# A decoder layer over 64 sequences: VectorE's chains in single calls, all call lists drawn up anew, two waits of GpSimd left out

## The chip, the cores and the metric

One core of a Trainium2 chip runs the whole kernel in one launch. The metric is the device time in microseconds, from the kernel's start to its end; lower is better. The engines of the core are named as the profile names them: PE (TensorE), DVE (VectorE), ACT (ScalarE), POOL (GpSimd) and SP (SyncE, whose queue carries the DMAs).

## The reference

Each of 64 sequences has 256 tokens of 256 channels (`x`) and a context of 120 tokens (`ctx`). All three parts end in a residual sum and a layer norm:

```python
# 1. mixer (a state-space layer, 8 heads of 64)
z, xBC, dt = split(x @ W_in.T)
dt  = softplus(dt + dt_bias)
xBC = silu(causal_conv4(xBC) + conv_b);  xs, B, C = split(xBC)
y   = ssd(xs * dt, -exp(A_log) * dt, B, C) + xs * D      # = (exp(segsum) * C B^T) (xs dt)
y   = y * silu(z);  y = y * rsqrt(mean(y*y) + 1e-5) * norm_w
x1  = layernorm(x + y @ W_out.T)
# 2. cross attention: queries from x1, keys and values from [ctx, x1] (376 rows), 8 heads
x2  = layernorm(x1 + softmax(q k^T / 8) v @ Wout)
# 3. coupling net, three cycles over all 256 channels of each token
gf  = sigmoid(gelu(gelu(mean_tokens(x2) @ g1) @ g2) @ g3)
out = x2
for _ in range(3):
    tf = sigmoid(gelu(gelu(gelu(out @ c1) @ c2) @ c3) @ c4)
    out = out + (0.1 + r * (0.7*gf + 0.3*tf - 0.5) * 2) * twist(out)
result = layernorm(out)
```

`twist` permutes the four quarters of the channels and changes two signs.

## The kernel before

All tensors of one sequence fit on the chip, so nothing is tiled over DMA beyond loading a sequence and storing it. The work is a software pipeline over sequences, written out by hand. In the iteration `p` of the steady loop the coupling net works on `f = p - 2`, attention on `a = p - 1`, the mixer on `m = p`, and the projections of `m + 1` are begun. Each engine has its own in-order list of calls: PE's loop is at L630 to L701, ACT's at L1195 to L1276, DVE's at L1929 to L2002, POOL's at L2296 to L2319, and SP's at L2457 to L2471, each between a list for the first sequences and one for the last. There is no scheduler: an engine runs its list from the top and stops wherever a semaphore that the call needs is not up. The semaphores count calls, so the same call may stand elsewhere in the list as long as its buffers allow.

PE writes to eight PSUM banks: bank 0 for the coupling net, a ring of three for scores, one of two for queries, keys, values and turned probabilities, one of two for the mixer (L234). A bank is free when the reader named in `freed` has counted up; with two or three banks a late reader on DVE or ACT stops PE two or three calls later.

The calls that the text speaks of, by PE's list:

- `scores(s, c, i)` (L418): four products of one head pair, which use 64 of the array's rows each (`r = slice(k * HD, (k + 1) * HD)`). DVE takes the row maximum (`top`, L1638), ACT exponentiates (`exp`, L979), PE turns the result (`turn`, L431), and ACT (L989) and DVE (L1657) take turns at copying it from PSUM.
- `values(s, c)` (L442) and `y_pair(s, q)` (L316): products that write 64 of the array's columns each.
- `layer(s, cyc, n)` (L479): layer `n` of the coupling net in cycle `cyc`; L497, L503 and L512 are its products, L1021, L1023 and L1025 ACT's gelus, L1033 the tanh that stands for the sigmoid. Between two cycles DVE runs `cycle` (L1708): the coupling (L1716), its product with the twisted part (L1721 or L1727), and the sum (L1724 or L1729). PE's next layer (L497) waits for the gelu of that sum (L1021).
- `x2_turn(s)` (L468, its instructions at L475): the start of the coupling net of a sequence, once per sequence.
- On DVE: `taps` (L1440, its instructions at L1442), three dependent additions of the convolution; `norm` (L1416), the statistics of a layer norm; `out_sum` (L1731), three dependent steps; and so on. In each of them a step waits for the one before it, on DVE itself.
- On POOL: `masked` (L2119), the causal mask over the decay matrix `Lm`; `times_g` (L2130), `Lm` times `C B^T`, which `y_pair` waits for; `factors` (L2198), the small numbers that `out_sum` needs; `ffn` and `att`, reciprocal roots for the layer norms.

Two waits on POOL have no data behind them. `times_g(m + 1, 0, summed=f)` waits until DVE has finished `out_sum(f, 1)`, and `factors(f, divided=a)` waits until DVE has multiplied the attention output by the reciprocals (L1666).

ACT holds one set of function tables at a time. The exponential, the gelu, the logarithm of softplus and the tanh with the exponential are in different sets, and where its list goes from one to another an `ACT_TABLE_LOAD` stands: seven in each sequence.

## Time and profile before

| | |
|---|---|
| median of 3 runs | 3865.07 us (3864.32 to 3865.35) |
| span of the profiled execution | 3861.4 us |
| around the span | 3.7 us against the median |
| PE, DVE, ACT, POOL busy | 98%, 85%, 84%, 45% |
| chain that ended last, by engine | PE 59%, ACT 16%, DVE 15%, POOL 4%, issue 4% |
| `ACT_TABLE_LOAD` | 1.283 us each, 189 ahead of `exp`, 125 ahead of the gelu |

The time of the profiled execution is its span of 3861.4 us and what lies around it; the median of the runs is 3.7 us above the span. The busy times of the engines come from the same execution. A busy share of 98% means that the engine had an instruction in it, not that every instruction took its least possible time: matmuls overlap, and the time from the start of one group to the start of the next is what a group costs.

### The profile page before, as it was taken

How to read it: one execution, taken by the hardware profiler on the slowest of the kernel's cores; microseconds unless marked ns; L12 is line 12 of the kernel's file. 1: busy time of each engine (PE TensorE's matmuls, PEld its weight loads, DVE VectorE, ACT ScalarE, POOL GpSimd, SP SyncE). 2: the span in 40 equal slices, each digit the busy share in tenths (PEclk: the TensorE clock that was granted, in tenths of full speed). 3: DMA queues.
4: the chain of work that ended last, by engine and by line, in shares of the span. 5: the costliest groups of instructions: out<-in, count | busy, mean ns of one | idle time of the engine just before them, and what ended most of it. 6: DMA issues, size and time to landing. Idle time of an engine off the chain costs nothing.

```text
span 3861.4 us, 77375 instructions
## 1 busy us (share of the span) xinstructions
PE 3783.3 (98%) x25728; PEld 3000.9 (78%) x25728; DVE 3286.2 (85%) x8098; ACT 3237.9 (84%) x7812; POOL 1748.5 (45%) x3084
## 2 busy tenths in 40 slices
PE   6999999999999999999999999999999999999997
...
GB/s 97 54 47 59 55 45 61 54 42 58 58 45 55 48 59 54 45 61 53 43 57 59 45 55 50 56 55 45 61 55 42 61 55 45 55 54 53 55 38 17
DMA packets 312350, 203.14 MB, mean 53 GB/s; under 512 B 55056, under 2 KB 310928, under 8 KB 311952
## 3 DMA queue, kind: packets, MB, share of 16 engines
...
## 4 chain that ended last, share of the span: by engine, by line
PE 59%; ACT 16%; DVE 15%; issue 4%; POOL 4%; DMA 1%; SPq 0%; DVEq 0%; POOLq 0%
PE psum L253 20%; PE psum L428 8%; PE psum L338 6%; PE psum L463 5%; PE psum L438 5%; PE psum L452 4%; PE psum L325 4%; ACT prob L979 3%; ACT h L1021 2%; ACT L979 2%; ACT L1021 2%; PE psum L497 2%; ACT xc L891 2%; POOL rs_mix L2175 2%; DVE nmax L1638 1%
## 5 line engine op out<-in xcount | busy, mean ns | idle before, releaser
L979 ACT ACTIVATE prob<-psum,nmax 128x376 f32<-128x376 f32 x1024 | 585.2, 575 | 49.5 <-DVE nmax L1638 46.2
L1638 DVE TENSOR_REDUCE nmax<-psum 128x1 f32<-128x376 f32 x1024 | 541.5, 540 | 14.4 <-PE psum L428 11.0
L2139 POOL TENSOR_TENSOR Lm<-Lm,G 128x384 f32<-128x384 f32 x512 | 506.1, 1012 | 92.8 <-DVE out_sb L1741 68.4
L438 PE MATMUL psum<-ident,prob 128*128 128x128 f32 (+1 forms) x3072 | 480.5, 276 | 2.1 <-ACT probT L989 1.1
L1442 DVE SCALAR_TENSOR_TENSOR u<-psum,par,u 128x253 f32<-128x253 f32 (+5 forms) x960 | 449.1, 479 | 28.1 <-ACT u L882 1.7
L428 PE MATMUL psum<-kT,q_sb 64*128 64x376 f32 x2048 | 467.7, 528 | 0.2 <-ACT prob L979 0.2
L438 PEld LDWEIGHTS psum<-ident,prob 128*128 128x128 f32 (+1 forms) x3072 | 363.0, 141 | 73.9 <-issue 45.0
L989 ACT ACTIVATE probT<-psum 128x384 f32<-128x384 f32 x512 | 252.7, 494 | 182.7 <-PE psum L438 182.5
L2126 POOL TENSOR_SCALAR_AFFINE_SELECT Lm<-Lm 128x256 f32<-128x256 f32 x512 | 205.7, 435 | 411.6 <-DMA Lm<-cum_row 411.6
L253 PE MATMUL psum<-x_hi,w_in_hi 128*128 128x256 f32 (+1 forms) x1152 | 360.9, 313 | 22.5 <-DVE w_in_lo L1764 9.3
L452 PE MATMUL psum<-probT,V 128*64 128x256 f32 (+1 forms) x3072 | 375.0, 385 | 0.3 <-ACT probT L989 0.3
L253 PE MATMUL psum<-x_hi,w_in_lo 128*128 128x256 f32 (+1 forms) x1152 | 326.0, 283 | 0.0
L253 PE MATMUL psum<-x_lo,w_in_hi 128*128 128x256 f32 (+1 forms) x1152 | 325.4, 283 | 0.0
L452 PEld LDWEIGHTS psum<-probT,V 128*64 128x64 f32 (+1 forms) x3072 | 202.4, 136 | 134.5 <-ACT probT L989 33.0
L1657 DVE COPY probT<-psum 128x384 f32<-128x384 f32 x512 | 279.9, 547 | 31.4 <-PE psum L438 27.2
L2194 POOL TENSOR_TENSOR h_a<-h_a,cpl 128x512 f32<-128x512 f32 x64 | 82.0, 1281 | 492.3 <-DVE h_pre L1724 492.3
L915 ACT ACTIVATE Lm<-Lm,ncum 128x256 f32<-128x256 f32 x512 | 262.8, 513 | 0.7 <-DVE ncum L1533 0.7
L463 PE MATMUL psum<-wo_sb,oT 128*128 128x256 f32 x1024 | 248.3, 386 | 0.7 <-DVE oT L1666 0.7
L979 ACT ACT_TABLE_LOAD x189 | 242.5, 1283 | 3.3
L338 PE MATMUL psum<-w_out_sb,g 128*128 128x256 f32 x1024 | 237.8, 386 | 0.0
L253 PEld LDWEIGHTS psum<-x_hi,w_in_hi 128*128 128x128 f32 (+1 forms) x1152 | 215.0, 187 | 28.4 <-issue 12.8
L463 PEld LDWEIGHTS psum<-wo_sb,oT 128*128 128x128 f32 x1024 | 189.4, 190 | 58.7 <-issue 32.9
...
## 6 DMA issues: line engine op xcount, KB each, us to landing
...
invT<-inv_row SPq DMA_DIRECT2D x256, 128.0 KB, 3.0
...
inv_row<-inv_t SPq DMA_DIRECT2D x512, 1.0 KB
...
```

The source lines that it names most:

```text
L253: t = mm(dst, a, b, start=n == 1, stop=n == 3 * KT)
L338: t = mm(banks[b][:, i * D:(i + 1) * D], g[:, c, i * P:(i + 1) * P], w_out_sb[:, c, :], start=c == 0, stop=c == CT - 1)
L428: mm(banks[b][:, 0:NK], q_sb[r, c, i * P:(i + 1) * P], kT[r, c, :], start=True, stop=True).then_inc(p_sc, 1)
L438: t = tr(banks[b][0:m, j * P:(j + 1) * P], prob[:, r, j0:j0 + m], ident[:, :])
L452: t = mm(banks[b][k * HD:(k + 1) * HD, 0:L], V[0:m, j, h * HD:(h + 1) * HD], probT[0:m, (8 * s + h) % HP, j, :], start=j == 0, stop=j == l ...
L463: t = mm(banks[b][:, 0:D], oT[:, c, i * P:(i + 1) * P], wo_sb[:, c, :], start=c == 0, stop=c == CT - 1)
L915: act(Lm[:, h, 0:L], Lm[:, h, 0:L], ACT.Exp, bias=ncum[:, 0, h:h + 1])
L979: act(prob[:, r, :], b[:, 0:NK], ACT.Exp, bias=nmax[:, n:n + 1], accum_out=psum_row[:, n:n + 1]).then_inc(a_exp, 1)
L1442: stt(u[0:rows, c, d:L], src[:, 0:L - d], prm("conv_w", 4 * c + 3 - d, slice(0, rows)), u[0:rows, c, d:L], ALU.mult, ALU.add).then_inc(don ...
L1638: e.tensor_reduce(nmax[:, n:n + 1], banks[bank_of["sc", s, n]][:, 0:NK], AX.X, ALU.max, negate=True).then_inc(d_max, 1)
L1657: cp(probT[:, (8 * s + 2 * c + k) % HP, :, i * P:(i + 1) * P], b[:, 0:len(JT) * P].rearrange("p (j t) -> p j t", j=len(JT))).then_inc(d_tn, 1)
L2139: t = tt(Lm[:, h, :], Lm[:, h, :], G[:, :], ALU.mult)
```

## The change

1. DVE's functions are cut into single instructions, each with the semaphore it needs: `taps` into `tap` (called by `conv_tap(s, c, n)` and `bcdt_tap(s, n)`), `norm` into `row_stats` and `row_mean`, `cycle` into `gain`, `twisted_part` and `pre`, `out_sum` into `out_x` and `out_tw`, and in the same way `cum`, `by_token`, `x1_raw`, `x1_norm`, `x1_keep`, `kv_split`, `inverse` and `x2_split`. Their arithmetic is the same, and so is the number of instructions.
2. The lists of all five engines, for the first sequences, the steady loop and the last ones, are written in another order. PE's steady list now begins at another place in the period. SP starts the load of the first context behind those of the weights.
3. The two waits of POOL are left out.
4. A few semaphores follow from it: a bank of `bcdt` is free only when its taps are done too, `conv_th` waits for two channels' own counts, and the first spreading of the sums waits for the weights.

```diff
-                freed[b] = [(d_dta, s + 1)]
+                freed[b] = [(d_dta, s + 1), (d_uB, 3 * s + 3)]
...
-            def taps(src, c, rows, done, at):
-                for n, d in enumerate((1, 2, 3)):
-                    stt(u[0:rows, c, d:L], src[:, 0:L - d], prm("conv_w", 4 * c + 3 - d, slice(0, rows)),
-                        u[0:rows, c, d:L], ALU.mult, ALU.add).then_inc(done, 1)
-                    if n < 2:
-                        ve.wait_ge(done, at + n + 1)
...
+            def tap(src, c, rows, n, done, s):
+
+                d = n + 1
+                ve.wait_ge(done, 3 * s + n)
+                stt(u[0:rows, c, d:L], src[:, 0:L - d], prm("conv_w", 4 * c + 3 - d, slice(0, rows)),
+                    u[0:rows, c, d:L], ALU.mult, ALU.add).then_inc(done, 1)
+
+            def bcdt_tap(s, n):
+                if not live(s):
+                    return
+                ve.wait_ge(a_uB, s + 1)
+                tap(banks[bank_of["bcdt", s]][0:TAIL, 0:L], CT, TAIL, n, d_uB, s)
...
-            def cycle(s, cyc):
-
-                if not live(s):
-                    return
-                n = FD * s + 3 * cyc
-                c_all = cpl[:, cyc, :].unsqueeze(1).broadcast_to([P, KT, L])
+            def gain(s, cyc):
+
+                if not live(s):
+                    return
                 ve.wait_ge(a_f, FA * s + 6 + 5 * cyc)
                 ve.wait_ge(d_base, s + 1)
                 ts(cpl[:, cyc, :], cpl[:, cyc, :], tf_gain[:, :], c_cyc[:, :], ALU.mult, ALU.add).then_inc(d_f, 1)
-                ve.wait_ge(d_f, n + 1)
+
+            def twisted_part(s, cyc):
+
+                if not live(s):
+                    return
+                ve.wait_ge(d_f, FD * s + 3 * cyc + 1)
+                ve.wait_ge(d_x2, 2 * s + 2)
+                ve.wait_ge(a_hb, s + 1)
+                c_all = cpl[:, cyc, :].unsqueeze(1).broadcast_to([P, KT, L])
                 if cyc == 0:
-                    ve.wait_ge(d_x2, 2 * s + 2)
-                    ve.wait_ge(a_hb, s + 1)
                     tt(h_pre[:, :, :], h_b[:, :, :], c_all, ALU.mult).then_inc(d_f, 1)
-                    ve.wait_ge(a_ha, s + 1)
-                    ve.wait_ge(d_f, n + 2)
-                    tt(h_pre[:, :, :], h_pre[:, :, :], h_a[:, :, :], ALU.add).then_inc(d_f, 1)
                 else:
                     ve.wait_ge(l_tw, 2 * s + 2)
                     tt(h_b[:, :, :], h_b[:, :, :], c_all, ALU.mult).then_inc(d_f, 1)
-                    ve.wait_ge(d_f, n + 2)
-                    tt(h_pre[:, :, :], h_pre[:, :, :], h_b[:, :, :], ALU.add).then_inc(d_f, 1)
-
-            def out_sum(s, i):
+
+            def pre(s, cyc):
+
+                if not live(s):
+                    return
+                ve.wait_ge(a_ha, s + 1)
+                ve.wait_ge(d_f, FD * s + 3 * cyc + 2)
+                tt(h_pre[:, :, :], h_pre[:, :, :], (h_b if cyc else h_a)[:, :, :], ALU.add).then_inc(d_f, 1)
...
+            def out_x(s, i):
...
+                ts(out_sb[:, i, :], x2[:, s % 2, i, :], of_x[:, i:i + 1], None, ALU.mult).then_inc(d_out[i], 1)
+
+            def out_tw(s, i, k):
+
+                if not live(s):
+                    return
+                ve.wait_ge(d_out[i], 3 * s + 1)
                 x2_, o = x2[:, s % 2, i, :], out_sb[:, i, :]
-                ts(o, x2_, of_x[:, i:i + 1], None, ALU.mult).then_inc(d_out[i], 1)
-                ve.wait_ge(d_out[i], 3 * s + 1)
-                stt(o[:, 0:P], x2_[:, P:D], of_tw[:, i:i + 1], o[:, 0:P], ALU.mult, ALU.add).then_inc(d_out[i], 1)
-                stt(o[:, P:D], x2_[:, 0:P], of_minus[:, i:i + 1], o[:, P:D], ALU.mult, ALU.add).then_inc(d_out[i], 1)
+                to, of_, by = ((slice(0, P), slice(P, D), of_tw), (slice(P, D), slice(0, P), of_minus))[k]
+                stt(o[:, to], x2_[:, of_], by[:, i:i + 1], o[:, to], ALU.mult, ALU.add).then_inc(d_out[i], 1)
...
-            def times_g(s, q, summed=None):
-
-                if not live(s):
-                    return
-                if summed is not None:
-                    po.wait_ge(d_out[1], 3 * summed + 3)
+            def times_g(s, q):
+
+                if not live(s):
+                    return
...
-            def factors(s, divided=None):
+            def factors(s):
...
-                if divided is not None:
-                    po.wait_ge(d_o, 2 * divided + 2)
...
                 sp.wait_ge(d_cum, s + 1)
+                sp.wait_ge(set_w, 3)
                 sp.wait_ge(cum_in, 32 * (s - 1))
```

PE, mid kernel, around the products of `Lm` (`y_pair`, L325 before and L326 now) and the scores (L428, now L429). Before:

```order
L438 MATMUL psum<-ident,prob 120x128
L438 MATMUL psum<-ident,prob 128x128 x2
L325 MATMUL psum<-Lm,xdt 64x256 x2
L325 MATMUL psum<-Lm,xdt 64x128 x2
L325 MATMUL psum<-Lm,xdt 64x256 x2
L325 MATMUL psum<-Lm,xdt 64x128 x2
L428 MATMUL psum<-kT,q_sb 128x376 x2
L438 MATMUL psum<-ident,prob 120x128
L438 MATMUL psum<-ident,prob 128x128 x2
L438 MATMUL psum<-ident,prob 120x128
L438 MATMUL psum<-ident,prob 128x128 x2
```

and now:

```order
L439 MATMUL psum<-ident,prob 128x128 x2
L429 MATMUL psum<-kT,q_sb 128x376 x2
L326 MATMUL psum<-Lm,xdt 64x256 x2
L326 MATMUL psum<-Lm,xdt 64x128 x2
L326 MATMUL psum<-Lm,xdt 64x256 x2
L326 MATMUL psum<-Lm,xdt 64x128 x2
L429 MATMUL psum<-kT,q_sb 128x376 x2
L326 MATMUL psum<-Lm,xdt 64x256 x2
L326 MATMUL psum<-Lm,xdt 64x128 x2
L326 MATMUL psum<-Lm,xdt 64x256 x2
L326 MATMUL psum<-Lm,xdt 64x128 x2
L429 MATMUL psum<-kT,q_sb 128x376 x2
```

Between the scores and the two halves of `y_pair`'s work no turn (L438, now L439) stands any more; seven calls that use half of the array follow one another.

DVE at the end of the coupling net's first cycle: `cpl`, `h_pre` are the coupling's, `u` is the convolution (L1442 before, L1451 now). Before:

```order
L1706 SCALAR_TENSOR_TENSOR c_cyc<-tg,gf_gain,c_base 128x1
L1716 TENSOR_SCALAR cpl<-cpl,tf_gain,c_cyc 128x256
L1721 TENSOR_TENSOR h_pre<-h_b,cpl 128x512
L1724 TENSOR_TENSOR h_pre<-h_pre,h_a 128x512
L1442 SCALAR_TENSOR_TENSOR u<-psum,par,u 128x255
L1442 SCALAR_TENSOR_TENSOR u<-psum,par,u 128x254
L1442 SCALAR_TENSOR_TENSOR u<-psum,par,u 128x253
L1442 SCALAR_TENSOR_TENSOR u<-psum,par,u 128x255
L1442 SCALAR_TENSOR_TENSOR u<-psum,par,u 128x254
L1442 SCALAR_TENSOR_TENSOR u<-psum,par,u 128x253
L1430 TENSOR_SCALAR ctx_n<-ctx_sb,mv_ctx,rs_ctx 120x256
```

and now:

```order
L1677 TENSOR_TENSOR kv_lo<-kv,kv_hi 128x2x256
L1670 CAST kv_hi<-kv 128x2x120
L1773 TENSOR_SCALAR cpl<-cpl,tf_gain,c_cyc 128x256
L1451 SCALAR_TENSOR_TENSOR u<-psum,par,u 128x255
L1677 TENSOR_TENSOR kv_lo<-kv,kv_hi 128x2x120
L1451 SCALAR_TENSOR_TENSOR u<-psum,par,u 128x255
L1784 TENSOR_TENSOR h_pre<-h_b,cpl 128x512
L1451 SCALAR_TENSOR_TENSOR u<-psum,par,u 128x254
L1795 TENSOR_TENSOR h_pre<-h_pre,h_a 128x512
L1451 SCALAR_TENSOR_TENSOR u<-psum,par,u 128x254
L1684 TENSOR_REDUCE nmax<-psum 128x1
L1451 SCALAR_TENSOR_TENSOR u<-psum,par,u 128x253
```

The two runs of three dependent taps are taken apart, and the steps of the coupling and of the split of `kv` stand between them.

ACT where the projections' softplus (`dt_e`) meets the first gelus (`h`, L1021 before and L1026 now). Before:

```order
L989 ACTIVATE probT<-psum 128x3x128
L870 ACTIVATE dt_e<-dt_e 8x256
L872 ACT_TABLE_LOAD
L872 ACTIVATE dt_e<-dt_e,ones 8x256
L1021 ACT_TABLE_LOAD
L1021 ACTIVATE h<-psum,par 128x256 x2
L969 ACTIVATE V<-psum 128x512
L1043 ACTIVATE h_a<-psum 128x512
L979 ACT_TABLE_LOAD
```

and now:

```order
L1012 ACTIVATE h_pre,x2sum<-psum 128x256 x2
L874 ACTIVATE dt_e<-dt_e 8x256
L876 ACT_TABLE_LOAD
L876 ACTIVATE dt_e<-dt_e,ones 8x256
L896 ACT_TABLE_LOAD
L896 ACTIVATE xc<-u 128x512
L984 ACTIVATE prob,psum_row<-psum,nmax 128x376
L1048 ACTIVATE h_a<-psum 128x512
L1063 ACT_TABLE_LOAD
L1063 ACTIVATE g<-psum,par 128x1
L1026 ACTIVATE h<-psum,par 128x256 x2
```

The first half of the convolution's tanh (`xc`, L896) now stands behind the softplus and needs a table of its own, so a sequence has eight table loads and not seven.

POOL behind the last of the factors (`of_minus`), where the two waits were. Before:

```order
L2225 TENSOR_SCALAR of_x<-of_x 128x2
L2226 TENSOR_SCALAR of_minus<-of_tw 128x2
L2139 TENSOR_TENSOR Lm<-Lm,G 128x384 x2
L2126 AFFINE_SELECT Lm<-Lm 128x2x128 x2
L2139 TENSOR_TENSOR Lm<-Lm,G 128x384 x2
L2115 TENSOR_SCALAR ve_ffn<-mv_ffn 128x1
L2117 TENSOR_TENSOR rs_ffn<-ve_ffn,minus_half 128x1
L2115 TENSOR_SCALAR ve_ffn<-mv_ffn 128x1
L2117 TENSOR_TENSOR rs_ffn<-ve_ffn,minus_half 128x1
L2139 TENSOR_TENSOR Lm<-Lm,G 128x384 x4
```

and now:

```order
L2529 TENSOR_SCALAR of_x<-of_x 128x2
L2530 TENSOR_SCALAR of_minus<-of_tw 128x2
L2445 TENSOR_TENSOR Lm<-Lm,G 128x384 x8
L2423 TENSOR_SCALAR ve_ffn<-mv_ffn 128x1
L2425 TENSOR_TENSOR rs_ffn<-ve_ffn,minus_half 128x1
L2455 TENSOR_TENSOR g<-xc,gate 128x256
L2423 TENSOR_SCALAR ve_ffn<-mv_ffn 128x1
L2425 TENSOR_TENSOR rs_ffn<-ve_ffn,minus_half 128x1
```

All eight products with `G` (L2139, now L2445) follow the factors in one run, and the masks stand before them.

## Rows read from the trace of the kernel before

**Rows 1.** Page, part 1: busy us, share of the span, instructions of each engine.

```profile
PE 3783.3 (98%) x25728; PEld 3000.9 (78%) x25728; DVE 3286.2 (85%) x8098; ACT 3237.9 (84%) x7812; POOL 1748.5 (45%) x3084
```

**Rows 2.** Windows: stretch, length, busy us (count) of PE, PEld, DVE, ACT, POOL, clock.

```profile
0.00:60.00 60.00, 30.78 (x148) 25.14 (x148) 45.13 (x116) 31.28 (x57) 22.07 (x39) 0.80 0.52 155
60.00:120.00 60.00, 52.94 (x345) 40.93 (x346) 45.78 (x113) 39.47 (x98) 22.20 (x31) 0.94 0.04 11
120.00:3780.00 3660.00, 3641.74 (x24920) 2892.27 (x24921) 3155.79 (x7776) 3128.46 (x7562) 1684.26 (x2960) 1.00 0.18 52
3780.00:3862.00 82.00, 57.88 (x319) 42.61 (x315) 39.54 (x95) 38.69 (x96) 19.97 (x54) 0.82 0.06 17
```

**Rows 3.** Turning of `x` into channels (L475): durations, first and last start, two stretches.

```profile
L475 PE MATMUL psum<-ident,x x4: 271/272/273, 146.0 to 146.3; 128*128 128x128 f32 x4
...
L475 PE MATMUL psum<-ident,x x8: 270/272/273, 3683.3 to 3741.4; 128*128 128x128 f32 x8
```

**Rows 4.** Waits of PE, largest group: line, releaser, us in total, times, longest.

```profile
PE psum L497 <- ACT h L1021: 19.0, 64, 3.6
```

**Rows 5.** Timeline of PE, mid kernel: start us, us, instruction, count [idle before <-releaser].

```profile
1516.91 1.52 PE L452 MATMUL psum<-probT,V 120*64 120x256 f32 x12
1518.36 0.38 PE L527 MATMUL psum<-g,gw_sb 128*128 128x1 f32 x2
...
1524.86 1.52 PE L452 MATMUL psum<-probT,V 120*64 120x256 f32 x12
1526.41 1.10 PE L497 MATMUL psum<-h,cw_sb 128*128 128x256 f32 x4
...
1528.81 0.49 PE L438 MATMUL psum<-ident,prob 128*120 128x128 f32 x3
1529.27 0.44 PE L253 MATMUL psum<-kv_hi,wkv_hi 128*128 128x376 f32 x1
...
1530.40 0.61 PE L512 MATMUL psum<-h,cw_row 128*128 128x128 f32 x4
1530.84 0.49 PE L438 MATMUL psum<-ident,prob 128*120 128x128 f32 x3
1531.09 0.36 PE L253 MATMUL psum<-x_hi,w_in_hi 128*128 128x256 f32 x1
...
1535.36 0.49 PE L438 MATMUL psum<-ident,prob 128*120 128x128 f32 x3
1536.04 1.10 PE L497 MATMUL psum<-h,cw_sb 128*128 128x256 f32 x4 [0.20 <-ACT h L1021]
...
1538.35 2.81 PE L452 MATMUL psum<-probT,V 120*64 120x256 f32 x24
1541.10 0.39 PE L509 MATMUL psum<-cw_col,h 128*128 128x2 f32 x2
```

**Rows 6.** Timeline of DVE, the same period.

```profile
1525.24 2.94 DVE L1442 SCALAR_TENSOR_TENSOR u<-psum,par,u 128x255 f32<-128x255 f32 x6
...
1528.41 0.73 DVE L1604 TENSOR_SCALAR x<-x_pre,mv_mix,rs_mix 128x256 f32<-128x256 f32 x2
...
1531.85 0.41 DVE L1716 TENSOR_SCALAR cpl<-cpl,tf_gain,c_cyc 128x256 f32<-128x256 f32 x1 [1.18 <-ACT cpl L1033]
1532.30 0.69 DVE L1727 TENSOR_TENSOR h_b<-h_b,cpl 128x512 f32<-128x512 f32 x1
```

**Rows 7.** Table loads of ACT at `exp`: count, busy us, mean ns, idle before.

```profile
L979 ACT ACT_TABLE_LOAD x189 | 242.5, 1283 | 3.3
```

**Rows 8.** Waits of POOL: the first of the two that the change concerns.

```profile
POOL c_col L2215 <- DVE oT L1666: 223.6, 61, 4.8
```

**Rows 9.** Page, part 5: products with `G` on POOL, with the second wait.

```profile
L2139 POOL TENSOR_TENSOR Lm<-Lm,G 128x384 f32<-128x384 f32 x512 | 506.1, 1012 | 92.8 <-DVE out_sb L1741 68.4
```

**Rows 10.** Groups of DVE, normalising calls of one shape: count, busy us, mean ns.

```profile
L1430 DVE TENSOR_SCALAR out_sb<-out_sb,mv_ffn,rs_ffn 128x256 f32<-128x256 f32 x128 | 93.7, 732 | 30.5 <-POOL rs_ffn L2117 30.5
...
L1430 DVE TENSOR_SCALAR x<-x,mv_att,rs_att 128x256 f32<-128x256 f32 x128 | 52.2, 408 | 1.2 <-POOL rs_att L2117 1.2
```

1807 lines of the change are left out of this document (1053 added, 754 removed).

## The prediction

> **What bounds the kernel now.** I read the page's busy shares first: PE is busy for 98% of the span, DVE for 85%, ACT for 84%, POOL for 45% [rows 1]. Next the windows, because a share over the whole span mixes the ends with the middle. In the 3660 us from 120 to 3780 PE is busy for 3641.74, so it is idle for 18; in the first 120 us it is idle for 29 + 7 = 36, in the last 82 for 24 [rows 2]. Then the period: the first `x2_turn` starts at 146.0, the 61st at 3683.3, so 60 periods take 3537.3 us and one takes 58.96 [rows 3]; the middle window holds 62 of them. Per period ACT is busy for 3128.46/62 = 50.5 and DVE for 3155.79/62 = 50.9: eight us of slack on each. The bound is PE's own list. The waits confirm it: the largest group, the first layer of a cycle behind ACT's gelu, is 19.0 us in 64 times [rows 4].
>
> So only two things can shorten the period: what PE's calls cost in their order, and the stalls still in it. The groups' start-to-start times show both, where durations don't, since matmuls overlap [rows 5]:
> - A head pair's values cost 1518.36 - 1516.91 = 1.45 us. Two values calls with nothing between them (x24) cost 1541.10 - 1538.35 = 2.75, not 2.90. Half-array calls next to each other save 0.15 per joint.
> - Stalls: values take 1.55 before the next layer and not 1.45 (0.10); the turn at 1528.81 takes 0.46 where the one at 1530.84 takes 0.25 (0.21: a bank is still held); the turn at 1535.36 takes 0.68, of which 0.25 is its own and 0.43 lies before the gelu, 0.20 of it named by the profile. Together 0.74 per period; other, smaller ones I can't tell from the calls' cost.
>
> **PE's new order.** I counted the half-array calls (scores, values, `y_pair`) in both steady lists, and how often they stand together. Before they form ten groups in a period: the scores of (0,1), (1,0), (1,1), (3,0) and (m,0,0) alone, `y_pair` 0 and 1 behind scores, `y_pair` 2 and 3 ahead of scores, scores with values 0, values 1 alone, values 2 and 3. Now there are six: values 2 and 3 with scores (0,1); scores (1,0); the seven calls around `y_pair`; scores (3,0); values 0 and 1 with scores (3,1); scores (m,0,0). Four groups fewer, at 0.15: 0.60 us less. The calls moved away from between them still run, and each starts behind a call of another kind as before, so I book nothing for them. That is 0.60 x 61 = 37 us.
>
> Below, this could be nothing, if the joint of the x24 row belongs to two values calls alone and scores beside `y_pair` save nothing (only two of the four joins are of values). Above, it is 0.7, if entering from a turn costs more than the 0.15.
>
> The Trainium skill speaks against part of it. "TensorEngine Tiling (Array Packing)", section Key Properties, says that changing the tiling mode, not only the tile, drains TensorE. Scores split the rows and values and `y_pair` split the columns, so by that rule a change between them inside a group costs too: three such changes before, six now. Counted in changes of any kind that is 23 before and 18 now, and the saving would be half of an entry-and-exit pair's 0.15 times five, 0.38 us per period or 23 us, not 37. No row shown here separates the two; it is a rival below.
>
> **The stalls.** The stall at 1536.04 sits on a chain. PE's third layer starts at 1530.40; DVE's coupling starts 1.45 later (1.18 of it idle, waiting for the tanh), its three steps of 0.41, 0.69 and again 0.69 with their gaps take 1.86 [rows 6]; then ACT loads a table, 1.28 [rows 7], computes the gelu, and PE starts 2.33 after DVE's last step: 5.64 in all. In the new list PE places other calls of 4.98 us between the same two layers (one K tile, two `xcT`, the next scores, two turns, a z projection, at their start-to-start times). If the table were loaded behind DVE's last step again, PE would stand still for 0.66. But between ACT's tanh and the gelu now stand only one K copy and one `exp`, so the load runs beside DVE's steps: 5.64 - 1.28 = 4.4 at best; with the K copy and the exponential waiting for PE's K tile it is nearer 4.9. I take a stall of 0.1 to 0.2 here. At the first gelu of the sequence ACT's list has become longer by one load (eight per sequence, one behind softplus): + 1.28 x 61 on ACT, which lifts it from 50.5 to 51.8 of 58 and hides in its slack except there; between `x2_turn`'s end and that layer PE has about 3.2 us of other calls, ACT about 2.8 with the load (both added up by me from the timelines of before, an estimate). So it is tight in two places, and loose in most others, because DVE answers sooner (next part). Of the 0.74 I take 0.5 to remain: -0.24 x 61 = -14 us.
>
> Bounds: all of it goes (-45 us), or the new order's own stalls are 0.3 us above the old (+18 us).
>
> **VectorE in single steps.** Six taps in two dependent runs take 2.94 us; two independent calls of 0.41 take 0.73 from start to end, a pitch of 0.32 against (2.94 - 0.48)/5 = 0.49 for calls of 0.48 [rows 6]. A neighbour that waits for the one before starts 0.01 behind its end; one that doesn't starts 0.08 ahead of it. That is about 0.1 per dependent pair. By my count some 33 pairs stand side by side in a period before and 5 now: 2.8 us of DVE's time per period. DVE is not the bound, so this alone is worth nothing; what it does is to bring row maxima and copies forward, and I have put that into the stalls. Cost if the cover fails: a step now spread over other instructions ends later than it did (the three taps of one channel now have six other instructions among them), which `conv_th` and the turns behind it would feel; the slack of eight us covers it.
>
> **GpSimd's two waits.** They cost POOL (223.6 + 68.4)/61 = 4.8 us per period [rows 8, 9], on an engine that is idle for more than half. What they kept apart is now together: eight products `Lm` x `G` of 1.01 us [rows 9], about 8 us in one run, start as DVE's `out_x` and `out_tw` do. DVE's normalising of `out_sb`, which ran beside such products, takes 732 ns on average, and the same call on `x`, which mostly didn't, 408 [rows 10]. If six DVE calls of a period each lose 0.3 so, DVE is 1.9 us later there, against 2.8 won. I book zero on PE, with the loss as the rival on the slower side.
>
> **The ends.** The first context is now loaded behind the weights, and DVE's first statistics wait for it; the casts of the query and key weights come early on ACT. PE's 36 us of idle in the first 120 hold both a gain and a loss: the later projections need no cast in the middle, the first taps may wait for the context. The closing chain behind the last `x2_turn` is the same. I take 0, bounds -8 and +8.
>
> **Sum.** 3861.4 - 37 - 14 + 0 = 3810.4, and with the 3.7 us by which the median stands above the profiled span, 3814; rounded for the smaller unnamed gains and losses I say 3815.
>
> **The rivals.**
> - *The stalls go altogether.* For it: DVE 2.8 us freer, POOL 4.8; against it: the two tight places on ACT. -(0.6 + 0.74) x 61 = -82: 3783.
> - *The gain is eaten or was never there.* Either each change of split inside a group costs as much (-23 and no stalls won: 3842), or the joins save only where values meet values and the gelu's chain, with its added load, holds the period near 58.9: about 3862, no change. This is also the case in which the change does not do what it says, since freeing DVE moves nothing that PE waits for.
> - *Slower.* POOL's one run of eight products lies on DVE's `out_x`, `out_tw`, the statistics and `x_low`. Behind these stand the row maxima for the scores of (1,0) and (1,1); the ring for scores has three banks, so PE stops as soon as DVE is later than about 1 us with a maximum. Six calls at up to 0.65 (twice the mean surcharge of 0.32, if half of the 128 calls of rows 10 were hit) are 4 us on DVE in that stretch, where the freed pairs give back little; beyond the 1 us that the ring covers, up to 3 us can reach PE. I take 1.3 of them: with 0.84 won elsewhere, +0.46 x 61 = +28, which is 3893. It decides from 0.84 + 0.13 = 0.97 us per period of new waits on. For it speaks the 732; against it, that in all of the old lists' periods PE never lost more than 0.43 us at one place though DVE waited 1.18 in it [rows 5, 6].
>   The Trainium skill, "SBUF — State Buffer", section "SBUF: two separate sides", calls the port pair shared by the two engines an exclusive lock that whoever starts first keeps for the whole instruction, for DVE calls with two SBUF inputs among others. By that, `out_tw` could wait for a whole product of 1 us each: four of them, 4 us, the same end of the scale.
>
> **Chances.** The forecast 0.52, stalls gone 0.15, gain eaten 0.19 (of it 0.13 faster, 0.06 no change), slower 0.14. A measurement tells 0.2%, 7.7 us, from no change, so: faster 0.80, same 0.06, slower 0.14. The range goes from the stall-free case, 3783, to just past no change, 3866; about 0.15 lies above it and 0.04 below.
>
> **What would show it.** The period between two `x2_turn` should be 58.1 us (58.96 - 0.84). Right or wrong step by step: the seven calls around `y_pair` start to start at their single costs less 0.15 a joint; the wait of the first layer behind the gelu, 19.0 us in all, smaller; eight table loads a sequence; DVE's busy time lower by some 2.8 x 62 = 170 us minus what POOL costs it (the pairs' gaps are short, so part shows as idle time instead); POOL's two waits gone and `out_x` and `out_tw` longer than before. The forecast is wrong if scores inside the long group start 0.1 or more late behind `y_pair`, if PE waits over 0.5 us a period for row maxima, or if DVE's calls beside the eight products take 0.7 us each.

## The result, and the profile after

The changed kernel takes 4256.33 us (median of 4 runs, 4248.81 to 4264.10) against 3864.70 of the kernel before: ratio 1.101, 95% interval 1.0996 to 1.103. It is slower by 391 us where 50 us less was forecast, and far above the range of 3783 to 3866.

The profiled execution is 4262.3 us long and the slowest of the four. First the page's part 1 and two windows (columns as in [rows 1, 2]):

```profile
PE 3826.6 (90%) x25728; PEld 3049.7 (72%) x25728; DVE 3508.3 (82%) x8098; ACT 3318.3 (78%) x7873; POOL 1782.4 (42%) x3084
```

```profile
0.00:60.00 60.00, 21.41 (x119) 18.21 (x120) 37.08 (x96) 26.76 (x52) 22.12 (x37) 1.00 0.39 117
120.00:4180.00 4060.00, 3696.76 (x24968) 2948.58 (x24967) 3385.31 (x7786) 3212.91 (x7631) 1716.86 (x2960) 0.99 0.16 47
```

PE is busy for 90% and not 98% [rows 1]; nothing became full. In the middle PE stood still for 363 of 4060 us, where it was 18 of 3660 [rows 2]. DVE's busy time rose by 222 us for the same 8098 instructions; some 170 us less was expected, minus what POOL costs. The starts of the coupling net (L476 now; the two stretches of [rows 3]):

```profile
L476 PE MATMUL psum<-ident,x x4: 270/272/273, 156.9 to 157.2; 128*128 128x128 f32 x4
```

and, near the end,

```profile
L476 PE MATMUL psum<-ident,x x12: 270/272/273, 4082.6 to 4187.1; 128*128 128x128 f32 x12
```

The first is 11 us later than before, the 61st at 4082.6: a period of (4082.6 - 156.9)/60 = 65.43 us, 6.47 above the 58.96 of before. Sixty such periods are 388 us; the head adds 11, the tail 2: together the 401 us between the two spans (the medians are 391 apart). So the loss is in the steady loop. The waits of PE say who ends the idle time (line, releaser, us in total, times, longest):

```profile
PE psum L439 <- DVE x L1726: 135.0, 59, 2.6
PE psum L498 <- ACT h L1026: 120.5, 66, 3.6
PE psum L313 <- DVE xc L1513: 56.3, 63, 1.6
```

Against 19.0 us for the largest group before [rows 4] there are three of 56 to 135, each about once per sequence: a turn that needs the bank of the output projection, which DVE's residual sum (L1726) frees; the third cycle's first layer behind the gelu; the mixer's transposes behind DVE's silu. In PE's timeline of one period they stand at three places:

```profile
2013.46 0.63 PE L313 MATMUL psum<-ident,xc 128*128 128x128 f32 x4 [0.72 <-DVE xc L1513]
...
2020.89 1.10 PE L498 MATMUL psum<-h,cw_sb 128*128 128x256 f32 x4 [1.84 <-ACT h L1026]
...
2025.08 2.82 PE L453 MATMUL psum<-probT,V 120*64 120x256 f32 x24
2027.83 0.90 PE L429 MATMUL psum<-kT,q_sb 64*128 64x376 f32 x4
...
2033.97 0.90 PE L429 MATMUL psum<-kT,q_sb 64*128 64x376 f32 x4
2037.43 0.54 PE L439 MATMUL psum<-ident,prob 128*120 128x128 f32 x3 [2.56 <-DVE x L1726]
...
2040.90 0.49 PE L439 MATMUL psum<-ident,prob 128*120 128x128 f32 x3
2041.32 0.90 PE L429 MATMUL psum<-kT,q_sb 64*128 64x376 f32 x4
2042.15 1.52 PE L326 MATMUL psum<-Lm,xdt 128*64 128x256 f32 x16
2043.60 0.90 PE L429 MATMUL psum<-kT,q_sb 64*128 64x376 f32 x4
```

All three end in DVE. DVE's timeline of the same period:

```profile
2010.27 0.89 DVE L1481 SCALAR_TENSOR_TENSOR th<-th,u 16x256 f32<-16x256 f32 x1
2011.17 1.42 DVE L1482 SCALAR_TENSOR_TENSOR th<-th,u 16x256 f32<-16x256 f32 x1
...
2017.94 0.41 DVE L1773 TENSOR_SCALAR cpl<-cpl,tf_gain,c_cyc 128x256 f32<-128x256 f32 x1
...
2026.74 0.69 DVE L1716 TENSOR_TENSOR oT<-oT,invT 128x512 f32<-128x512 f32 x1 [2.85 <-DMA invT<-inv_row]
2029.22 0.69 DVE L1716 TENSOR_TENSOR oT<-oT,invT 128x512 f32<-128x512 f32 x1 [1.78 <-ACT oT L1003]
...
2030.94 1.07 DVE L1803 TENSOR_SCALAR out_sb<-x,of_x 128x256 f32<-128x256 f32 x1 [0.57 <-POOL of_minus L2530]
2032.05 0.97 DVE L1812 SCALAR_TENSOR_TENSOR out_sb<-x,of_tw,out_sb 128x128 f32<-128x128 f32 x1
2032.95 1.08 DVE L1812 SCALAR_TENSOR_TENSOR out_sb<-x,of_minus,out_sb 128x128 f32<-128x128 f32 x1
...
2035.08 0.96 DVE L1812 SCALAR_TENSOR_TENSOR out_sb<-x,of_tw,out_sb 128x128 f32<-128x128 f32 x1
2035.96 0.41 DVE L1426 BATCH_NORM_STATS2 st_ffn<-out_sb 128x6 f32<-128x256 f32 x1
2036.30 0.74 DVE L1812 SCALAR_TENSOR_TENSOR out_sb<-x,of_minus,out_sb 128x128 f32<-128x128 f32 x1
2036.96 0.74 DVE L1726 TENSOR_TENSOR x<-psum,x 128x256 f32<-128x256 f32 x2
```

and POOL's:

```profile
2009.60 1.28 POOL L2500 TENSOR_TENSOR h_a<-h_a,cpl 128x512 f32<-128x512 f32 x1
2010.96 1.35 POOL L2502 TENSOR_TENSOR h_b<-h_b,h_a 128x512 f32<-128x512 f32 x1
...
2030.87 7.03 POOL L2445 TENSOR_TENSOR Lm<-Lm,G 128x384 f32<-128x384 f32 x7
```

Read them side by side. From 2030.87 POOL runs seven products on end; DVE's six calls of the output sum take 0.74 to 1.08 us each, about one per product, while a call of the statistics between them (L1426) takes its usual 0.41, and the residual sum starts at 2036.96. (The eighth product waits 4 us for ACT.) From 2009.60 POOL runs the twist; DVE's two silu calls take 0.89 and 1.42. And from 2024 to 2029 DVE, whose list has come to the division, stands still twice. The groups over the whole span, of after and then of the kernel before (count, busy us, mean ns, idle before):

```profile
L1803 DVE TENSOR_SCALAR out_sb<-x,of_x 128x256 f32<-128x256 f32 x128 | 125.3, 980 | 26.8 <-POOL of_minus L2530 26.0
L1812 DVE SCALAR_TENSOR_TENSOR out_sb<-x,of_tw,out_sb 128x128 f32<-128x128 f32 x128 | 118.1, 924 | 4.3
L1812 DVE SCALAR_TENSOR_TENSOR out_sb<-x,of_minus,out_sb 128x128 f32<-128x128 f32 x128 | 111.7, 873 | 0.0
...
L1482 DVE SCALAR_TENSOR_TENSOR th<-th,u 16x256 f32<-16x256 f32 x64 | 85.9, 1342 | 0.9
...
L1481 DVE SCALAR_TENSOR_TENSOR th<-th,u 16x256 f32<-16x256 f32 x64 | 62.7, 979 | 1.0 <-ACT th L868 1.0
```

```profile
L1741 DVE SCALAR_TENSOR_TENSOR out_sb<-x,of_minus,out_sb 128x128 f32<-128x128 f32 x128 | 53.8, 420 | 0.0
...
L1740 DVE SCALAR_TENSOR_TENSOR out_sb<-x,of_tw,out_sb 128x128 f32<-128x128 f32 x128 | 47.1, 368 | 4.6
L1738 DVE TENSOR_SCALAR out_sb<-x,of_x 128x256 f32<-128x256 f32 x128 | 46.9, 367 | 76.4 <-POOL of_minus L2226 76.3
...
L1473 DVE SCALAR_TENSOR_TENSOR th<-th,u 16x256 f32<-16x256 f32 x64 | 26.7, 417 | 0.9
L1472 DVE SCALAR_TENSOR_TENSOR th<-th,u 16x256 f32<-16x256 f32 x64 | 26.1, 408 | 0.0
```

The output sum costs 355.1 us where it cost 147.8, the two silu calls 148.6 where they cost 52.8: 207 and 96 us, 4.7 us per sequence of VectorE's time, paid for leaving GpSimd's work beside it.

Behind its long waits PE also loses clock. In another period it stood still for 1.83 us until 1628.55 and for 2.46 until 1646.32, and the windows behind show the granted clock at its lower level, 1.2 GHz instead of 2.4 (columns as above, the clock third from the end):

```profile
1630.20:1633.40 3.20, 3.20 (x17) 3.20 (x16) 1.01 (x2) 2.02 (x4) 0.35 (x2) 0.50 0.48 125
1647.30:1650.50 3.20, 3.20 (x14) 3.20 (x14) 3.20 (x12) 1.93 (x6) 0.00 (x0) 0.50 0.02 5
```

In the trace of before there is no such stretch between 120 us and the 61st `x2_turn`; here 24 of the 60 periods have one or more and last 66.11 us on average, the other 36 last 64.97. An estimate from the two: (65.43 - 64.97) x 60, some 28 of the 401 us, go with the clock. No run separates them from the waits in front of them.

### The profile page after: what moved, and what is told of

The parts are those of the page before. It is cut to its first block, busy times and chain, and to the rows that moved or that the text cites. A ratio compares the mean times of both kernels' runs of the same rounds, so it can differ in the third digit from the quotient of the medians.

```text
span 4262.3 us, 77876 instructions
## 1 busy us (share of the span) xinstructions
PE 3826.6 (90%) x25728; PEld 3049.7 (72%) x25728; DVE 3508.3 (82%) x8098; ACT 3318.3 (78%) x7873; POOL 1782.4 (42%) x3084
## 4 chain that ended last, share of the span: by engine, by line
PE 55%; DVE 26%; issue 7%; ACT 5%; SPq 3%; DMA 2%; POOL 2%; POOLq 0%; DVEq 0%; ACTq 0%
PE psum L254 19%; PE psum L439 7%; PE psum L429 7%; PE psum L339 5%; DVE out_sb L1812 5%; PE psum L326 4%; PE psum L453 4%; DVE out_sb L1803 3%; PE psum L498 3%; DMA invT<-inv_row 2%; DVE probT L1707 2%; SPq L2706 1%; PE psum L504 1%; DVE th L1481 1%; DVE xc L1513 1%
## 5 line engine op out<-in xcount | busy, mean ns | idle before, releaser
L439 PE MATMUL psum<-ident,prob 128*128 128x128 f32 (+1 forms) x3072 | 517.0, 285 | 136.8 <-DVE x L1726 135.0
L2445 POOL TENSOR_TENSOR Lm<-Lm,G 128x384 f32<-128x384 f32 x512 | 518.5, 1042 | 286.3 <-ACT Lm L921 267.8
L1684 DVE TENSOR_REDUCE nmax<-psum 128x1 f32<-128x376 f32 x1024 | 548.3, 536 | 46.3 <-PE psum L429 44.0
L439 PEld LDWEIGHTS psum<-ident,prob 128*128 128x128 f32 (+1 forms) x3072 | 360.7, 146 | 295.9 <-DVE x L1726 172.1
L429 PE MATMUL psum<-kT,q_sb 64*128 64x376 f32 x2048 | 483.5, 528 | 0.5 <-ACT kT L965 0.5
L1451 DVE SCALAR_TENSOR_TENSOR u<-psum,par,u 128x255 f32<-128x255 f32 (+5 forms) x960 | 433.0, 468 | 35.2 <-ACT u L886 29.3
L2434 POOL TENSOR_SCALAR_AFFINE_SELECT Lm<-Lm 128x256 f32<-128x256 f32 x512 | 227.0, 481 | 541.4 <-DMA Lm<-cum_row 541.4
L254 PE MATMUL psum<-x_hi,w_in_hi 128*128 128x256 f32 (+1 forms) x1152 | 355.1, 308 | 24.9 <-DVE u L1451 10.8
L453 PE MATMUL psum<-probT,V 128*64 128x256 f32 (+1 forms) x3072 | 360.8, 383 | 2.2 <-ACT probT L994 2.2
L1716 DVE TENSOR_TENSOR oT<-oT,invT 128x512 f32<-128x512 f32 x128 | 91.9, 718 | 319.1 <-DMA invT<-inv_row 245.1
L2515 POOL TENSOR_TENSOR cd<-c_col 128x2 f32<-128x2 f32 x64 | 12.5, 196 | 734.3 <-DMA c_col<-c_row 734.3
L498 PE MATMUL psum<-h,cw_sb 128*128 128x256 f32 x768 | 210.6, 397 | 120.7 <-ACT h L1026 120.5
L429 PEld LDWEIGHTS psum<-kT,q_sb 64*128 64x128 f32 x2048 | 172.0, 184 | 126.9 <-issue 93.4
```

What stands on the lines that cost most here:

```text
L254: t = mm(dst, a, b, start=n == 1, stop=n == 3 * KT)
L429: mm(banks[b][:, 0:NK], q_sb[r, c, i * P:(i + 1) * P], kT[r, c, :], start=True, stop=True).then_inc(p_sc, 1)
L439: t = tr(banks[b][0:m, j * P:(j + 1) * P], prob[:, r, j0:j0 + m], ident[:, :])
L453: t = mm(banks[b][k * HD:(k + 1) * HD, 0:L], V[0:m, j, h * HD:(h + 1) * HD], probT[0:m, (8 * s + h) % HP, j, :], start=j == 0, stop=j == l ...
L498: t = mm(b[:, 0:L], cw2_sb[:, k, :], h1[:, k, :], start=k == 0, stop=k == KT - 1)
L1451: stt(u[0:rows, c, d:L], src[:, 0:L - d], prm("conv_w", 4 * c + 3 - d, slice(0, rows)), u[0:rows, c, d:L], ALU.mult, ALU.add).then_inc(don ...
```

## The experiments

Each ran beside the kernel before on the same chip, which took 3863.9 to 3865.5 us. Most are medians of two executions that lie up to 14.5 us apart (e4), so differences of a few us between two of them say nothing. "Less" and "slower" are against the changed kernel or the run that is named. Edits are shown in part, without the context.

**Waits put back (e1).**

```diff
+                if summed is not None and summed >= 0:
+                    po.wait_ge(d_out[1], 3 * summed + 3)
...
+                if divided is not None and divided >= 0:
+                    po.wait_ge(d_o, 2 * divided + 2)
```

> The changed kernel with GpSimd's two waits put back where they stood: its first product of a sequence waits for the first half of the output sum, and its factors wait for the division. Theory A (the waits kept GpSimd's products off VectorE's output sum; without them the six calls take 0.87 to 0.98 us instead of 0.37 to 0.42, 3.2 us a period, and the turn behind the residual sum stands still for 2.4): three of six calls are short again, some 1.6 us of 65.5 a period come back, but the factors start 1 us later because the division itself is late, so 0.5 to 1.5 us a period or 30 to 90 us less: 4170 to 4230. Theory B (the lists themselves put the division too late, behind a DMA that SyncE issues late, and this sets the period): no gain or a loss up to 1.3 us a period, 4256 to 4335.

4156.11 us, 100 less: somewhat more than theory A asked for. The division and the factors come late, but four of the six calls are short again, the three that the wait covers and the one that starts before the first product; the other two take 0.97 and 0.74 us in the timeline.

**Products behind both halves (e2).**

```diff
+                    po.wait_ge(d_out[1], 3 * summed + 3)
+                    po.wait_ge(d_out[0], 3 * summed + 3)
```

> The changed kernel with one wait for GpSimd: its eight products start only when both halves of VectorE's output sum are done; the factors don't wait. Theory A: the six calls of the output sum are back at 0.37 to 0.42 us, VectorE is 3.2 us earlier at the residual sum, the stall of the turn behind it (2.4 us a period) goes: 2.0 to 3.0 us a period less, 4070 to 4135. Theory B: VectorE catches up elsewhere and PE stands still at the next late place, 4220 to 4256; slower than 4256 if the products now come too late for the mixer's products.

4096.63 us, 160 less, inside theory A's range. The six calls are short, and the wait of 135 us for the residual sum is gone from the list of PE's waits; the gelu's stays:

```profile
L1803 DVE TENSOR_SCALAR out_sb<-x,of_x 128x256 f32<-128x256 f32 x128 | 45.4, 356 | 30.7 <-POOL of_minus L2533 30.1
```

```profile
PE psum L498 <- ACT h L1026: 120.8, 66, 3.6
```

**The two waits left out of the old lists (e3).**

```diff
-                factors(f, divided=a)
+                factors(f)
-                times_g(m + 1, 0, summed=f)
+                times_g(m + 1, 0)
```

> The kernel before with nothing changed but GpSimd's two waits left out (the third part of the change alone). Theory A: the output sum's six calls get slower here too, by up to 2 us a period where the old list has only two products in a row, and VectorE's slack takes half: 3865 to 3980, with the output sum's mean above 0.5 us. Theory B: the waits matter little in either order, 3855 to 3875.

3871.57 us, ratio 1.0018 (1.0006 to 1.0029). The output sum does get slower (589, 359 and 728 ns on average), but PE loses only 7 us. In the old list two products stand there, in the new one eight.

**Thin products (e4).**

```diff
-                    t = tt(Lm[:, h, :], Lm[:, h, :], G[:, :], ALU.mult)
+                    t = tt(Lm[:, h, 0:8], Lm[:, h, 0:8], G[:, 0:8], ALU.mult)
```

> The changed kernel with GpSimd's eight products per sequence cut to 8 of their 384 columns (the rest of the product with C B^T is left out, so the result is another): it takes away nearly all that they can hold VectorE up with, and makes them early. Theory A: output sum back at 0.37 to 0.42 us, 2.4 to 3.2 us a period less, 4060 to 4110. Theory B: 4220 or more. What remains above 58 us a period in this run is the price of the lists and of the other GpSimd work.

4056.37 us: 200 less. Of these 160 are what e2 gives back. No run splits the other 40: here the products also come early, and `x_low` (L1445), which e2's late products hold up to 1218 ns on average, takes 681.

**Reciprocals early (e5), on top of e2.** In SP's list:

```diff
                 spread_cum(a)
+                spread_inv(f - 1, 0)
...
-                spread_inv(f - 1, 0)
                 load_x(a)
```

> As e2_products_later (4097 us; output sum undisturbed), and SyncE issues the spreading of the first half of the attention reciprocals right behind that of the decay sums, some 30 us earlier, instead of behind the coupling rows. Theory A (where the transfers for the division stand in SyncE's list sets the division, which holds VectorE): VectorE's wait for them, 216 us in all, goes and 1 to 2 us a period with it: 3980 to 4040. Theory B (the division would wait for ACT's copy of the attention output and the output sum for the factors anyway): VectorE's wait moves to those, PE gains at most its 0.3 at the output projection: 4075 to 4097.

4096.77 us: no change, as theory B said. DVE's wait has another name:

```profile
DVE oT L1716 <- ACT oT L1003: 297.9, 62, 5.7
```

The division would have waited for ACT's copy of the attention output anyway.

**Twist first (e6), on top of e2.** In POOL's list:

```diff
+                twist(f - 2)
                 masked(a, 0)
...
                 masked(a, 3)
-                twist(f - 2)
```

> As e2_products_later, and GpSimd computes the two steps of the twist before the masks and not behind them, so that they no longer lie on VectorE's two calls for silu of B and C (0.96 and 1.34 us where they took 0.41 and 0.42). Theory A (this is the same contention, at a second place): the two calls are back near 0.42, PE's wait of 1.0 us a period at the mixer's transposes goes and some of the 2.0 us before the third cycle's first layer: 1.0 to 2.0 us a period, 3975 to 4035. Theory B (the order of VectorE's list sets both): under 0.3 us a period, 4080 to 4097.

4060.32 us, 36 less than e2: little more than half of the least that theory A gave. PE's wait at the transposes (L313) is gone from its list. The two calls fall to 576 and 526 ns, not to 0.42: the masks now lie on them.

**Coupling first (e7), on top of e2.**

```diff
                 by_token(a)
-                bc_high(a)
-                x1_keep(f, 0)
                 x_dt(a, 0)
-                bc_low(a)
                 gain(f - 2, 1)
                 twisted_part(f - 2, 1)
                 pre(f - 2, 1)
+                bc_high(a)
+                x1_keep(f, 0)
+                bc_low(a)
```

> As e2_products_later, and in VectorE's list the three steps of the second cycle's coupling stand ahead of the splitting of B and C (eight small calls) and not behind it. Theory A (contention alone): the chain to the gelu still starts late, under 0.5 us a period, 4065 to 4097. Theory B (VectorE's list asks for the coupling 2.5 us later than ACT has its tanh ready, and PE's 2.0 us before the third cycle's first layer are the price): 1.5 to 2.2 us a period less, 3960 to 4005, with PE's wait for the gelu near the 19 us of the kernel before.

4051.14 us, 45 less than e2, half of the least that theory B gave. PE's wait for the gelu went from 120.8 us to 11.9, below the 19 of the kernel before; but a new one took most of it:

```profile
PE psum L303 <- DVE xdt L1576: 72.6, 60, 2.2
```

Part of the 45 is the clock: from 120 to 4000 us the granted clock is 1.00 here and 0.99 in e2. e2's periods without a stretch at the lower clock last 62.18 us and e7's 61.85, 0.33 less, where the means of all periods differ by 0.78 (62.69 and 61.91).

**The three together (e8).** The edits of e5, e6 and e7 on top of e2.

> The edits of e5, e6 and e7 together on top of e2. If they are separate places the gains add up: the known stalls left are then those before the mixer's output projection (0.5 to 0.9 us), before a K tile (0.4) and small ones, so 59.5 us a period and 3890 to 3930. If they hide one another, it is no better than the best of the three by more than 20 us.

4029.71 us: 67 below e2, where the single gains are 0, 36 and 45. It missed the 3890 to 3930 of adding up; by the other branch of the expectation, the places hide one another. The wait at L303 is now 105.1 us: what is called earlier makes something else late. Whether DVE is simply full there, e12 decides.

**Dependent neighbours taken apart in the old lists (e9).** Taps of two channels alternate; `gain`, the twisted part and the sum stand between taps; the two steps of `x2_split` stand between the taps of B, C and dt.

```diff
-                bcdt(m + 1)
-                x2_split(f)
+                bcdt_and_split(m + 1, f)
                 softplus(m + 1)
-                conv(m + 1, 0)
-                conv(m + 1, 1)
+                conv_two(m + 1, 0)
...
-                cycle(f, 0)
-                conv(m + 1, 2)
-                conv(m + 1, 3)
+                cycle_and_conv(f, m + 1)
```

> The kernel before, with all its lists, where only VectorE's dependent neighbours are taken apart in the steady loop: the taps of two channels alternate, the coupling's three steps stand between taps, the split of x2 between the taps of B, C and dt (14 of some 33 dependent pairs a period). The first part of the change alone. Theory A (VectorE isn't the bound; its freed 1 to 1.5 us a period are worth nothing to PE): within 0.1%, 3861 to 3869. Theory B (the kernel before loses time to these pairs on the chain to the gelu): 0.2 to 0.35 us a period less, 3843 to 3852.

4021.88 us, ratio 1.040 (1.0387 to 1.0422): 156 us slower than the kernel before, and neither theory had it. DVE's timeline:

```profile
1992.58 0.43 DVE L1734 CAST x2T_hi<-h_pre 128x512 fp32r<-128x512 f32 x1 [1.51 <-ACT h_pre L1007]
...
1994.92 1.27 DVE L1461 SCALAR_TENSOR_TENSOR dt_e<-dt_a 8x256 f32<-8x256 f32 x1
...
2012.87 0.41 DVE L1779 TENSOR_SCALAR cpl<-cpl,tf_gain,c_cyc 128x256 f32<-128x256 f32 x1 [1.34 <-ACT u L882]
```

The cast of `x2` was put between two taps and waits 1.51 us for ACT, and the two taps that could have run wait behind it. The coupling was put behind the wait for the convolution's input, 1.34 us. And what came later met GpSimd: L1461 takes 1.27 us for its 0.42. PE's wait for the gelu (L497) is 125.9 us where it was 19.0.

**Seven table loads (e10), on top of e8.** On ACT, and on DVE (`x_silu`):

```diff
-                conv_th(m + 1, 0)
-                exp(a, 11)
                 keep_a(f)
...
                 layer(f, 0, 2)
+                exp(a, 11)
+                conv_th(m + 1, 0)
                 exp(a, 12)
...
-                x_silu(a, 0)
...
                 kv_low(f, 1)
+                x_silu(a, 0)
```

> As e8_three (4030 us), with ACT's exponential 11 and the first tanh of the convolution moved behind the first gelus, so that a sequence has seven table loads again. Theory A (the added load hides in ACT's slack): 4010 to 4045. Theory B (it is on the path at the first gelu): 1.0 to 1.3 us a period less, 3950 to 3970.

4095.52 us: 66 slower than e8, outside both ranges. The load is one fewer, but DVE's silu moved into its full stretch, and PE has a new wait of 0.8 us a period (51.2 in 62 times) at a turn, for ACT's copy of the attention output (L1003). The load's own price stays open, since three calls moved with it.

**Thin products and twist (e11).** As e4, and both steps of `twist` on 8 columns (the first of them shown):

```diff
-                tt(h_a[:, :, :], h_a[:, :, :], cpl[:, 0, :].unsqueeze(1).broadcast_to([P, KT, L]), ALU.mult).then_inc(l_tw, 1)
+                tt(h_a[:, :, 0:8], h_a[:, :, 0:8], cpl[:, 0, 0:8].unsqueeze(1).broadcast_to([P, KT, 8]), ALU.mult).then_inc(l_tw, 1)
```

> The changed kernel with GpSimd's eight products and the two steps of the twist cut to 8 columns (the rest of both is left out, so the result is another). It shows what the new lists cost when GpSimd holds VectorE up at neither place. Theory A (contention is most of the loss): 3870 to 3950. Theory B (the lists cost at least as much: VectorE asks for the second coupling late and stands still before the division): 3990 to 4050, with PE's waits before the third cycle's first layer still over 1 us a period.

3952.93 us: 303 less. It lies between the two ranges, 3 us above theory A's. PE's wait for the gelu is still 95.8 us, as theory B said. So 303 of 391 us go with GpSimd's wide work (an upper bound for contention, since its results also come earlier, which may be up to the 40 us between e4 and e2), and 88 remain.

**Operands first (e12), on top of e8.** On DVE:

```diff
                 pre(f - 2, 1)
+                x_dt(a, 1)
                 bc_high(a)
-                x1_keep(f, 0)
                 bc_low(a)
+                x1_keep(f, 0)
...
-                x_dt(a, 1)
                 gate_silu(a, 0)
```

> As e8_three, where PE's largest wait (2.0 us a period) is for a bank that VectorE's second product with dt frees: that product, and the splitting of B and C, now stand right behind the coupling and ahead of the reciprocals and the first row maximum. If the order of VectorE's list is what costs: 0.8 to 1.2 us a period less, 3960 to 3985. If VectorE is simply full in this stretch (some 20 us of calls on end), the wait moves to the next call: 4000 to 4035.

3963.65 us: 66 less than e8, inside the first range. The wait at L303 is gone, so the order of DVE's list was the cause, and DVE was not simply full. Of the new lists with nothing left out only e17 is as fast; both are 2.5% behind the kernel before.

**Alternating taps alone (e13).** In the old lists, `conv(m + 1, 2j)` and `conv(m + 1, 2j + 1)` become one call whose taps alternate.

```diff
+                for k in range(6):
+                    c, d = 2 * j + k % 2, k // 2 + 1
+                    if k > 1:
+                        ve.wait_ge(d_u, 12 * s + 6 * j + k - 1)
```

> The kernel before, where only the taps of two channels alternate in the steady loop (eight dependent pairs a period taken apart, no call moved past another kind). In e9_old_lists_interleaved the six taps took 2.43 us and not 2.94, so 1.0 us of VectorE's time a period is freed. Theory A (e9 lost its 156 us to calls that were set before a wait, x2's split behind a tap and the coupling behind ACT's input of the convolution; freed time alone moves nothing): 3861 to 3868. Theory B (earlier taps bring VectorE's later calls to the gelu's chain or the scores forward): 3845 to 3858. Theory C (alternation itself does harm, as by meeting GpSimd at other calls): over 3872.

3859.94 us, ratio 0.9987 (0.9978 to 0.9997): 5 us faster than the kernel before, the fastest of all, at the edge of what can be told from none, and between the ranges of theories A and B. The six taps:

```profile
1991.71 2.42 DVE L1499 SCALAR_TENSOR_TENSOR u<-psum,par,u 128x255 f32<-128x255 f32 x6
```

against 2.94 us in [rows 6]: 0.52 us for four dependent neighbours taken apart, 0.13 each where a tenth was booked. Alternation does no harm, which leaves theory A's reading of e9: calls set ahead of a wait do.

**Thin GpSimd, coupling and operands first (e14).** The edits of e7 and e12 on top of e11.

> As e11_thin_gpsimd (3953 us; products and twist cut to 8 columns), and in VectorE's list the coupling, the second product with dt and the splitting of B and C stand first, as in e12. If VectorE's list was all that was left besides the contention, PE's 1.6 us a period before the third cycle's first layer go and the new PE order shows its worth: 3830 to 3870. If the waits around the division and the mixer's output projection (0.65 and 0.75 us a period) and new ones remain: 3870 to 3910.

4027.36 us: 74 slower than e11, and above both ranges. The gelu's wait went, and PE waits 108.3 us for the division. SP's timeline (DMA issues) shows the way of the reciprocals:

```profile
2033.41 2.15 SPq L2696 DMA_DIRECT2D inv_row<-inv_t  x4
...
2036.08 1.24 SPq L2706 DMA_DIRECT2D invT<-inv_row  x2
2037.37 0.61 SPq L2672 DMA_DIRECT2D x_sb<-in_x  x1
2038.02 0.46 SPq L2666 DMA_DIRECT2D xT_sb<-in_xT  x1
2038.59 1.24 SPq L2706 DMA_DIRECT2D invT<-inv_row  x2
```

They are ready later, because the coupling stands first; then the queue writes them out, reads the first half, loads two unrelated tensors, and reads the second half.

**Values side by side (e15), old lists.** On PE, and likewise `values_out` on ACT:

```diff
                 scores(a, 3, 1)
-                values(a, 0)
                 glob(f, 1)
...
                 q_pair(m, 0)
+                values(a, 0)
                 values(a, 1)
```

> The kernel before, where PE's list runs values 0 directly ahead of values 1, as the changed kernel does, and ACT's copies follow in the same way; nothing else is moved. It tests the one term that was booked as a gain. Theory A (half-array calls side by side save 0.15 to 0.2 us a joint): 9 to 12 us less, 3852 to 3857. Theory B (the later first values hold a bank or its copy, and PE waits for more than the joint saves): 3865 or more.

3976.23 us, ratio 1.0287: 111 slower than the kernel before. Theory B, which gave no size. What PE waits for:

```profile
PE psum L527 <- ACT g L1058: 66.2, 61, 1.1
PE psum L452 <- ACT q_sb L952: 40.3, 61, 0.7
```

The values call had covered ACT's gelu ahead of the global net's second product; without it PE waits 1.1 us there, and 0.7 between the two values for a bank.

**Thin GpSimd, reciprocals first too (e16).** On top of e14, on DVE and on SP:

```diff
                 pre(f - 2, 1)
+                inverse(f - 1, 1)
                 x_dt(a, 1)
+                turn_inverse(f - 1, 1)
...
                 spread_cum(a)
+                spread_inv(f - 1, 0)
...
-                spread_inv(f - 1, 0)
+                spread_inv(f - 1, 1)
                 load_x(a)
                 load_xT(m)
-                spread_inv(f - 1, 1)
```

> As e14_thin_and_first (4027 us; products and twist cut to 8 columns), with the attention's second reciprocals right behind the coupling on VectorE and both spreadings of the reciprocals ahead of the loads in SyncE's list. In e14 9.5 us pass between the reciprocals and the second division, VectorE stands for 6.8 of them, and PE waits 2.1 us a period at the output projection. If this queue was what ate the gain of the earlier coupling: 2 to 2.8 us a period less, 3855 to 3905, level with the kernel before. If not: over 3950.

3899.27 us: 128 less than e14, inside the first range. With GpSimd's wide work cut, the calls of e14 and these four moved, the new order is within 35 us of the old one.

**The same with nothing left out (e17), on top of e12.**

> As e12_operands_first (3964 us, nothing left out), with the same two edits. The place of the reciprocals costs PE 0.5 us a period there (output projection) and 0.3 at a K tile: 3915 to 3955. If GpSimd's masks and late products are what holds it: 3955 to 3975.

3962.30 us, no different from e12. The moves are those of e16, on top of e12, whose `spread_inv(f - 1, 0)` stands early already. The second range: with the masks and the late products whole, the reciprocals aren't the limit. No full form of the new lists beats the kernel before.

## Why the prediction was wrong

**The bound.** Read rightly for before: PE, with 8 us of slack on DVE and ACT. What failed is the use of it. The text took slack per period for cover at every place ("the slack of eight us covers it"). These lists are in order. In the new ones DVE stands still for 10.9 us a period; 5.0 of them are in front of the division (319.1 us in all, 12.0 before), where it can do nothing else, and the 19 us ahead of that hold less than 1 us of idle time. In that stretch there was next to no slack: e7, e8 and e14 show a call that is moved forward making another late, and e12 shows the order inside it to be worth 66 us.

**GpSimd's two waits.** This is the step that failed first and most: "I book zero on PE", because DVE would be "1.9 us later there, against 2.8 won". The six calls cost DVE 3.2 us more per sequence (207/64) at one place, and what the single steps won elsewhere didn't come back there. On PE it measured 160 us (e2). With the twist, which the new order laid on DVE's silu (1.5 us per sequence, not named in the text), and the products' later end, it is up to 303 (e11). The rival on the slower side named the mechanism and, but for the statistics, the calls. Its price for DVE was even high: 0.65 a call and 4 us for six, against 0.54 and 3.2. What it mis-sized is how much reaches PE, "1.3 of them", and where: not at row maxima, but 2.6 us at one turn (3.46 from the scores at 2033.97 to the turn, of which 0.83 are their own), since the bank is freed by the residual sum behind all six calls. So it came to 28 us over the kernel before. The Trainium skill's rule, which stood beside it ("SBUF — State Buffer", section "SBUF: two separate sides": whoever starts first keeps the pair for the whole instruction), is borne out in the timeline, where about one DVE call goes with one product; the four `out_tw` calls lost 2.0 us a sequence by it, half of the 4 that the prediction drew from it. Of the signs of being wrong that the prediction named, the last came true: DVE's calls beside the products take 0.87 to 0.98 us on average, over the 0.7 it set.

**Whether the waits alone mattered.** Not in the old order (e3: 7 us). The loss is the two edits together: waits given up, and seven of eight products without a pause where they had guarded.

**The stalls.** Booked at 14 us less, they became some 340 more (363 us of idle time on PE in the middle, where it was 18). Of the two tight places named on ACT, one became the second largest wait, 2.0 us a period before the third cycle's first layer; but the reason given (a table load) was not it: the load ends 1.9 us before the gelu starts, and e7 took the wait away by moving DVE's three steps, with the load still there. The prediction worked out the chain's length on ACT and never asked when DVE's list comes to the coupling: at 2017.94 it is 2.9 us behind ACT's tanh. The wait at the turn (2.3) and at the transposes (0.9) were not on its list. Those two are contention (e2, e6).

**PE's order.** 37 us were booked for four joins. In the timeline above a turn ahead of scores costs 0.42 (2040.90 to 2041.32) and one ahead of a full-array product 0.25 [rows 5]; scores cost 0.83 whether `y_pair`, a turn or a projection follows, and `y_pair` 1.45 ahead of scores or of a turn. So each group fewer saves an entry of 0.17, four of them 0.68, near the 0.60 booked. The rule of "TensorEngine Tiling (Array Packing)" of the Trainium skill, section Key Properties, that any change of mode drains, shows at the border to the full array. Between the two kinds of split the rows don't decide: two values calls cost 2.75 whether scores (2025.08 to 2027.83) or another call [rows 5] follow, and a second values call adds only 1.30 to the 1.45 of the first, so going from values to scores costs as much as leaving the half array. The rival with 23 us stays open. No run shows any of this as time, and e15, which tried one join alone, lost 111 us because the moved call had been cover.

**VectorE's single steps.** 0.1 us per pair: about right, 0.13 (e13). "This alone is worth nothing": right within 5 us. "What it does is to bring row maxima and copies forward": wrong; a finer list has more places at which a call can stand ahead of its data, and all behind it wait (e9).

**The ends.** 0 with 8 on either side; it was 13 more (11 at the head, 2 at the tail), outside the bounds. No run takes the head apart.
